# Four images through attention on one Trainium2 core: an image's head projections move up one output block, and the last LayerNorm is done in halves

## The chip, the cores and the metric

The kernel runs on one core of a Trainium2 chip. Times are microseconds (us) of device time for one launch, the median of several runs; the trace is that of one profiled execution.

## The reference

Four images of 256 channels and 32 x 32 pixels (N = 1024 tokens each) pass through three layers. Cut to what matters here:

```
q, k, v = wq x, wk x, wv x                     # layer 0: one attention of 1024 x 1024 per image
x = gamma * (v softmax(q^T k, axis=1)) + x
t = tokens(x)                                  # [4, 1024, 256]
h = groupnorm(layernorm(t)) * scale + bias     # layer 1: LayerNorm per token, GroupNorm per 8 channels
qkv = h w_qkv + b_qkv                          # 8 heads of 32
t = t + layernorm(t) + attention(q, k, v) w_proj + b_proj
t = t + expert(layernorm(t))                   # layer 2: one of 8 experts per token
```

Every softmax needs the maxima of its score rows before the exponentials; the kernel computes each score twice, once for the maxima and once for the exponentials.

## The kernel before, in words

The program is a sequence of four phases, each a block with its own instruction streams for TensorE (PE), VectorE (DVE), ScalarE (ACT), GpSimd (POOL) and the DMA queue of SyncE (SP). A phase starts when all engines have left the one before. The order in which each engine works is written out by hand, and semaphores (`wait_ge`) keep the engines apart; an engine works its stream in that order. `conv_phase` (layer 0 of all images, and layer 1 up to q, k and v), `head_phase` (32 attentions, four images times eight heads), `output_phase` and `expert_phase` follow each other.

In `conv_phase` a token block is 128 tokens, and an image has NB = 8 of them. For image b the stages are: `project` (q and k), `maxima` (8 blocks, two matmuls each into `ps_m`, reduced by DVE), `max_turn` (the maxima are transposed, and ACT and two small transfers put them as a row under the stacked keys), `scores` with ACT's exponentials, and then the output loop: `outputs(b, j)` for j = 0 to 7, eight matmuls into `ps_v`, after which DVE's `residual(b, j)` divides, adds the input and takes the LayerNorm statistics of the block. After the loop DVE's `first_norm(b)` normalizes all eight blocks into `lnt`.

Two other works are woven into image b's output loop. One is the next image's `maxima(b + 1, j)`, one block per j. The other is the layer-1 work of the image before, b - 1, by two tables, `precedes` and `follows`, indexed by j: `norms` part 0 (transposition of `lnt` into `ps_e`, statistics for GroupNorm), part 1 and part 2 (two tiny matmuls with `gmat` that sum over the channels of a group, each between short DVE chains that end in the scale and shift `gab`), ACT's `heads_in` (the normalized `h_c`, its rounded copy `h_hi`), DVE's `split_h` (the rest, `h_lo`), four `heads_qk` of 12 matmuls each, whose results ACT (`hi`) and DVE (`lo`) take from `ps_e` and SP spills to `qk_scr`, and two `heads_v` (48 matmuls in all), stored to `v_scr`. For the last image nothing follows, so this work is done after the loop (`last_image`), one part after another, and between the parts stand the first 14 (`LEAD`) blocks of maxima of head 0 and head 1 of the head phase (`hd.maxima`, `hd.block_max`); their operands, image 0's heads 0 and 1, are loaded during image 2's loop. Each `hd.maxima` waits until DVE has reduced the block before it, for it writes the same two banks of `ps_m`.

The tables of before, on PE:

```
precedes = {2: [(norms, 1)], 3: [(norms, 2)]}
follows = {0: [(norms, 0)], 5: [(heads_qk, 0), (heads_qk, 1)], 6: [(heads_qk, 2), (heads_qk, 3)],
           7: [(heads_v, 0), (heads_v, 1)]}
```

Of the kernel before, what the change touches and what calls it, by code (L numbers as in the profile page):

```python
# [27 lines left out]
ALU = mybir.AluOpType  # L28
# [88 lines left out]
def layer_norm(nc, st, done, lnt, res, mv, var, rstd, tmp):  # L117

    st.did(nc.vector.tensor_scalar(var[:, :], mv[:, :, 1], LN_EPS, None, ALU.add))
    st.wait()  # L120
    rsqrt(nc, st, rstd[:, :], var[:, :], tmp[:, :])
    for j in range(NB):
# [5 lines left out]
def moments(nc, st, mv, bst, pause):  # L128


    st.wait()
    nc.vector.memset(pause[:, :], 0.0)
    for j in range(NB):
        st.did(nc.vector.bn_aggr(mv[:, j, :], bst[:, j, :]))
# [119 lines left out]
def conv_phase(nc, io, keep, hd):  # L254
# [5 lines left out]
    with ExitStack() as ctx:  # L260
# [50 lines left out]
        a_whi, v_wlo, a_hhi, v_hlo = sem("a_whi", "v_wlo", "a_hhi", "v_hlo")  # L311
        PIECES = 4

        HEAD_BLOCKS = (2, 2, 2, 2, 2, 1, 1, 1, 1)
        assert sum(HEAD_BLOCKS) == LEAD

# [11 lines left out]
        with nc.Block() as block:  # L328

            @block.sync  # L330
            def _(sp):
# [103 lines left out]
            def _(act):  # L435
# [32 lines left out]
                def heads_in(b):  # L468

                    act.wait_ge(v_gab, b + 1)  # L470
# [5 lines left out]
                    for t in range(CT):  # L476
                        nc.scalar.activation(h_c[:, t, :], flat(ps_e[t]), ACT.Identity,
                                             scale=gab[:, 0, t:t + 1], bias=gab[:, 1, t:t + 1]).then_inc(a_h, 1)
                        act.wait_ge(a_h, 2 * b + t + 1)
                        nc.scalar.activation(h_hi[:, t, :], h_c[:, t, :], ACT.Copy).then_inc(a_hhi, 1)  # L480
                    for it in range(4):
                        if b == B - 1 and it == 3:
                            hd.row_hi(act, ps_v[:, 0, :], 0, 0, first=True)
# [26 lines left out]
            def _(pe):  # L510
# [87 lines left out]
                def norms(b, part):  # L598
# [5 lines left out]
                    else:  # L604

                        if b + 2 < B:
                            pe.wait_ge(v_max, 2 * (NB * (b + 2) + part + 1))
                        elif b == B - 1:
                            pe.wait_ge(hd.v_max, 2 * sum(HEAD_BLOCKS[:part]))
# [5 lines left out]
                def heads_qk(b, it):  # L615

                    pe.wait_ge(a_hhi, 2 * b + 2)
                    if b == 0 and it == 0:
# [39 lines left out]
                for b in range(-1, B):  # L658
                    for j in range(NB if b >= 0 else 0):
# [4 lines left out]
                        if b + 1 < B and not (b and j == NB - 1):  # L664
                            maxima(b + 1, j)
                        if b and b + 1 < B and j == NB - 1:
# [16 lines left out]
                last_image = [(norms, n) for n in range(3)] + [(heads_qk, n) for n in range(4)] + [(heads_v, n) for n in range(2)]  # L683
                for i, (part, n) in enumerate(last_image):
                    part(B - 1, n)
                    first = sum(HEAD_BLOCKS[:i])
                    for g in range(first, first + HEAD_BLOCKS[i]):
                        if g % NB == 0:
                            pe.wait_ge(*hd.loaded(hd.stack_in, 16 * STACK_DMAS, 0, g // NB))
                        if g == 0:  # L690
                            pe.wait_ge(v_max, 2 * NB * B)
                        hd.maxima(pe, ps_m, g, g // NB, g % NB, first=(g == 0))
                    if (part, n) == (heads_qk, 2):

                        pe.wait_ge(v_res0, NB * B)
                        hd.max_turn(pe, ps_v[:, 0, :], ident, 0, 0)

            @block.vector
            def _(dve):
# [46 lines left out]

                def first_norm(b):
# [46 lines left out]
                def split_h(b):  # L794

                    for t in range(CT):
                        dve.wait_ge(a_hhi, 2 * b + t + 1)
                        if b:
# [20 lines left out]
                precedes = {2: [(norms, 1)], 3: [(norms, 2)]}  # L819
                follows = {0: [(norms, 0)], 4: [(lambda b, n: split_h(b), 0)], 5: [(heads_qk, 0), (heads_qk, 1)], 6: [(heads_qk, 2), (heads_qk, 3)],  # L820
                           7: [(heads_v, 0), (heads_v, 1)]}
# [8 lines left out]
                for b in range(B):  # L830
                    for j in range(NB):
# [14 lines left out]
                    first_norm(b)  # L846
                    if b + 2 < B:
                        project(b + 2)
                last_image = [(norms, n) for n in range(3)] + [(heads_qk, n) for n in range(4)] + [(heads_v, n) for n in range(2)]
                for i, (part, n) in enumerate(last_image):  # L850
                    part(B - 1, n)
                    first = sum(HEAD_BLOCKS[:i])
                    for g in range(first, first + HEAD_BLOCKS[i]):
# [996 lines left out]
```

## Time and profile before

| | |
|---|---|
| median of 3 runs | 1238.78 us (1238.21 to 1240.36) |
| the profiled execution | 1240.58 us, its span 1238.8 us |
| PE busy | 1124.2 us, 91% of the span |
| DVE busy | 676.7 us, 55% |
| POOL busy | 570.6 us, 46% |
| ACT busy | 434.1 us, 35% |
| mean granted TensorE clock | 0.945 of full speed |

The shares are means over four phases; the change lies in the first, which ends at about 352.8 us of the span. The profile's own chain of waits, followed back from the end, does not reach that far, so the stage has to be read from the timelines of its engines.

### The profile page before, as it was taken

How to read it: one execution, taken by the hardware profiler on the slowest of the kernel's cores; microseconds unless marked ns; L12 is line 12 of the kernel's file. 1: busy time of each engine (PE TensorE's matmuls, PEld its weight loads, DVE VectorE, ACT ScalarE, POOL GpSimd, SP SyncE). 2: the span in 40 equal slices, each digit the busy share in tenths (PEclk: the TensorE clock that was granted, in tenths of full speed). 3: DMA queues.
4: the chain of work that ended last, by engine and by line, in shares of the span. 5: the costliest groups of instructions: out<-in, count | busy, mean ns of one | idle time of the engine just before them, and what ended most of it. 6: DMA issues, size and time to landing. Idle time of an engine off the chain costs nothing. (4 is left out here: it accounts for less than half of the span.)

```text
span 1238.8 us, 23452 instructions
## 1 busy us (share of the span) xinstructions
PE 1124.2 (91%) x7604; PEld 822.3 (66%) x7605; DVE 676.7 (55%) x1491; ACT 434.1 (35%) x511; POOL 570.6 (46%) x565
## 2 busy tenths in 40 slices
PE   6899999896679999999999999998726999999995
PEld 3577878685455555555555555556516999999994
DVE  4264747556467777777777777715742333333331
ACT  1303232320225555555555555564420111111110
POOL 0003030303047777877787878840361444444443
PEclk8799999897689999999999999998857999999998
DMA  6204361323152232323232323134455565565551
GB/s 210 60 1 128 135 188 68 119 87 131 73 167 76 80 94 60 94 60 94 60 94 67 101 68 100 31 121 136 149 118 175 194 215 193 191 203 208 191 193 61
DMA packets 61608, 148.44 MB, mean 120 GB/s; under 512 B 11360, under 2 KB 31776, under 8 KB 59904
## 3 DMA queue, kind: packets, MB, share of 16 engines
q1 hardware_dynamic: 53184, 123.39, 31.1%
q0 software_dynamic: 7536, 22.96, 5.6%
q10 hardware_dynamic: 848, 1.58, 0.5%
q8 instruction: 23, 0.38, 0.1%
q14 instruction: 17, 0.14, 0.0%
HBM read 104.58 MB, written 39.87 MB: 117 GB/s over the span
## 5 line engine op out<-in xcount | busy, mean ns | idle before, releaser
L217 DVE TENSOR_REDUCE s_nmax<-ps_v 128x1 f32<-128x512 f32 x484 | 311.3, 685 | 114.2 <-PE ps_v L211 104.0
L967 POOL TENSOR_TENSOR h_added<-h_added,h_expd 128x1024 f32<-128x1024 f32 x124 | 295.5, 2383 | 37.6 <-ACT h_expd L990 29.7
L990 ACT ACTIVATE h_expd<-ps_v 128x1024 f32<-128x1024 f32 x128 | 131.1, 1025 | 155.5 <-PE ps_v L1016 150.0
L1713 PEld LDWEIGHTS ps_h<-xs_c,lnt 128*128 128x128 f32 x1248 | 147.0, 194 | 4.8 <-issue 2.9
L1713 PE MATMUL ps_h<-xs_c,lnt 128*128 128x128 f32 x1248 | 147.5, 277 | 2.3 <-DVE xs_c L1665 2.3
L1723 PE MATMUL ps_y<-w,vals_t 128*128 x624 | 141.2, 379 | 0.6 <-DVE ys L1678 0.6
L1030 PE MATMUL h_ps_o<-h_expd,s_vh 128*32 128x256 f32 x2048 | 137.8, 387 | 0.0
L424 POOL TENSOR_TENSOR a_res<-a_res,a_lnt 128x2048 f32<-128x2048 f32 x4 | 18.2, 4539 | 253.0 <-DVE a_lnt L123 253.0
L990 ACT ACTIVATE h_expd<-h_ps_e 128x1024 f32<-128x1024 f32 x128 | 130.3, 1018 | 0.0
L1754 ACT ACTIVATE vals_t<-ps_h 128x1024 f32<-128x1024 f32 x39 | 39.9, 1024 | 255.8 <-DVE ps_h L1658 255.8
L1723 PEld LDWEIGHTS ps_y<-w,vals_t 128*128 128x128 f32 x624 | 115.5, 190 | 15.1 <-issue 1.0
L594 PE MATMUL a_ps_v<-a_val,a_expd 128*128 128x257 f32 x512 | 120.2, 388 | 5.1 <-ACT a_expd L464 4.5
L1658 DVE TENSOR_TENSOR ps_h<-ps_h,b_t 128x1024 f32<-128x1024 f32 x39 | 48.1, 1232 | 130.3 <-PE ps_h L1713 130.3
L594 PEld LDWEIGHTS a_ps_v<-a_val,a_expd 128*128 128x128 f32 x512 | 98.2, 194 | 23.5 <-ACT a_expd L464 6.5
L1555 POOL TENSOR_TENSOR pause<-pause 128x1 f32<-128x1 f32 x156 | 30.6, 196 | 156.0 <-DVE ys L1678 131.5
L967 POOL TENSOR_TENSOR h_added<-h_expd 128x1024 f32<-128x1024 f32 x31 | 73.8, 2380 | 56.2 <-ACT h_expd L990 56.2
L1030 PEld LDWEIGHTS h_ps_o<-h_expd,s_vh 128*32 128x32 f32 x2048 | 53.7, 109 | 52.0 <-issue 22.5
L715 DVE TENSOR_REDUCE a_nmax<-a_ps_m 128x1 f32<-128x512 f32 x64 | 41.2, 685 | 62.7 <-PE a_ps_m L554 62.7
L211 PE MATMUL ps_v<-s_stk2m,s_stk2n 96*128 96x512 f32 x128 | 51.9, 453 | 3.2 <-issue 3.1
L1176 POOL DMA_INDIRECT xs_scr<-lnt,pos x32 | 31.4, 982 | 50.6 <-DVE pos L1417 41.4
L211 PE MATMUL ps_v<-s_stk3m,s_stk3n 96*128 96x512 f32 x128 | 51.4, 446 | 0.0
L211 PE MATMUL ps_v<-s_stk1m,s_stk1n 96*128 96x512 f32 x116 | 46.6, 446 | 0.0
(222 smaller groups left out, 1592.2 us busy)
## 6 DMA issues: line engine op xcount, KB each, us to landing
lnt<-in_w SPq DMA_DIRECT2D x38, 1024.0 KB, 4.9
qk_scr<-a_head_hi SPq DMA_DIRECT2D x16, 512.0 KB, 2.6
qk_scr<-a_head_lo SPq DMA_DIRECT2D x16, 512.0 KB, 3.6
w<-in_w SPq DMA_DIRECT2D x8, 1024.0 KB, 5.9
xs<-xs_scr SPq DMA_DIRECT2D x39, 128.5 KB, 2.1
a_x_t<-in_x_t POOLq DMA_DIRECT2D x4, 1024.0 KB, 9.2
r_scr<-a_res POOLq DMA_DIRECT2D x4, 1024.0 KB, 6.1
v_scr<-res SPq DMA_DIRECT2D x4, 1024.0 KB, 3.8
```

Source lines behind the costliest of these rows:

```text
L211: self.nc.tensor.matmul(ps_m[:, half, :], n_st[0:STACK, nb * P:(nb + 1) * P], m_st[0:STACK, half * HALF:(half + 1) * HALF], start=True, st ...
L217: self.nc.vector.tensor_reduce(self.nmax[k][:, nb, half:half + 1], ps_m[:, half, :], AX.X, ALU.max, negate=True).then_inc(self.v_max, 1)
L594: last = nc.tensor.matmul(ps_v[:, j % 2, 0:C + 1], expd[:, m, j * P:(j + 1) * P], val[b % 2][:, m, :], start=(m == 0), stop=(m == NB - 1))
L715: nc.vector.tensor_reduce(nmax[b % 2][:, nb, half:half + 1], ps_m[:, half, :], AX.X, ALU.max, negate=True).then_inc(v_max, 1)
L967: nc.gpsimd.tensor_tensor(total[:, :], (expd[:, 0, :] if m == 1 else total[:, :]), expd[:, m, :], ALU.add).then_inc(g_add, 1)
L990: nc.scalar.activation(expd[:, m, :], flat(ps_e[m % 2]), ACT.Exp, scale=SCALE).then_inc(a_exp, 1)
L1030: mm = nc.tensor.matmul(ps_o[j % 2][q * D:(q + 1) * D, 0:QUARTER], vh[j % SLOTS][:, m, :], expd[:, m, q * QUARTER:(q + 1) * QUARTER], star ...
L1176: pool.indirect_dma_start(io["xs_scr"][:, :], bass.IndirectOffsetOnAxis(ap=keep["pos"][:, i:i + 1], axis=0), keep["lnt"][:, i, :], None).t ...
L1658: nc.vector.tensor_tensor(blocks, blocks, b1_t[:, bass.ds(e, 1), :].rearrange("p o (k n) -> p (o k) n", n=1).to_broadcast([P, KC, P]), ALU ...
L1713: last = nc.tensor.matmul(ps_h[k][:, c // 4, c % 4 * P:(c % 4 + 1) * P], w1_now[k][:, t, c * P:(c + 1) * P], xs_c[:, t, :], start=(t == 0) ...
L1723: last = nc.tensor.matmul(ps_y[:, 0:C], hid_t[k][:, c, :], w2[:, bass.ds(e, 1), c, :].rearrange("p o n -> p (o n)"), start=(c == 0), stop= ...
L1754: nc.scalar.activation(hid_t[k].rearrange("p k n -> p (k n)"), flat(ps_h[k]), ACT.Gelu).then_inc(a_gelu, 1)
```

## The change

Five edits, all in `conv_phase`:

- The layer-1 work of image b - 1 moves up one output block of image b: `norms` 1 and 2 stand before j = 1 and 2 instead of 2 and 3, `heads_qk` after j = 4 and 5, `heads_v` after j = 6 instead of 7; DVE's `split_h` after j = 3.
- The last image's `first_norm` becomes two halves of four token blocks: `norm_half(0)` on DVE after j = 5 of its own output loop, `norm_half(1)` after the loop; PE transposes each half on its own (`turn_half`).
- The eight blocks of head 0's maxima move from behind the last image's loop into it, one after each of j = 0 to 5 and two after j = 6 (`HEAD_BLOCKS`). Head 1's six blocks stay behind the loop: two after `norms` 2, one after each `heads_qk` (`TAIL_BLOCKS`). Head 0's row of maxima is therefore finished earlier, and SP writes it before the last image's first spill instead of before its fourth.
- ACT computes the rounded tile `h_hi` from PSUM with the same scale and shift as `h_c`, not as a copy of `h_c`, and before it; `heads_qk` 0 and 1 now also wait for `h_c`, which reads the bank that they overwrite.
- The waits before `norms` 1 and 2 are renumbered for the new places.

```diff
-def layer_norm(nc, st, done, lnt, res, mv, var, rstd, tmp):
+def layer_norm(nc, st, done, lnt, res, mv, var, rstd, tmp, blocks=range(NB)):
...
-        HEAD_BLOCKS = (2, 2, 2, 2, 2, 1, 1, 1, 1)
+        HEAD_BLOCKS = (1, 1, 1, 1, 1, 1, 2, 0)
+        TAIL_BLOCKS = {("norms", 2): 2, ("qk", 0): 1, ("qk", 1): 1, ("qk", 2): 1, ("qk", 3): 1}
+        HALVES = (range(0, NB // 2), range(NB // 2, NB))
...
-                        if b == B - 1 and it == 3:
+                        if b == B - 1 and it == 0:
                             hd.max_rows(sp, 0, 0)
...
-                        nc.scalar.activation(h_c[:, t, :], flat(ps_e[t]), ACT.Identity,
-                                             scale=gab[:, 0, t:t + 1], bias=gab[:, 1, t:t + 1]).then_inc(a_h, 1)
-                        act.wait_ge(a_h, 2 * b + t + 1)
-                        nc.scalar.activation(h_hi[:, t, :], h_c[:, t, :], ACT.Copy).then_inc(a_hhi, 1)
+                        for h, done in ((h_hi, a_hhi), (h_c, a_h)):
+                            nc.scalar.activation(h[:, t, :], flat(ps_e[t]), ACT.Identity,
+                                                 scale=gab[:, 0, t:t + 1], bias=gab[:, 1, t:t + 1]).then_inc(done, 1)
...
+                def turn_half(half):
+                    pe.wait_ge(*((v_lnh, 1), (v_ln, B))[half])
+                    if half == 0:
+                        pe.wait_ge(v_v1, 2 * (B - 1))
+                    for t in range(CT):
+                        for j in HALVES[half]:
+                            last = nc.tensor.transpose(ps_e[t][:, half, j % 4 * P:(j % 4 + 1) * P], lnt[:, j, t * P:(t + 1) * P], ident[:, :])
+                        last.then_inc(pe_lnh, 1)
...
-                precedes = {2: [(norms, 1)], 3: [(norms, 2)]}
-                follows = {0: [(norms, 0)], 5: [(heads_qk, 0), (heads_qk, 1)], 6: [(heads_qk, 2), (heads_qk, 3)],
-                           7: [(heads_v, 0), (heads_v, 1)]}
+                precedes = {1: [(norms, 1)], 2: [(norms, 2)]}
+                follows = {0: [(norms, 0)], 4: [(heads_qk, 0), (heads_qk, 1)], 5: [(heads_qk, 2), (heads_qk, 3)],
+                           6: [(heads_v, 0), (heads_v, 1)]}
...
+                        if b == B - 1:
+                            head_blocks(sum(HEAD_BLOCKS[:j]), HEAD_BLOCKS[j])
...
+                turn_half(0)
+                pe.wait_ge(v_res0, NB * B)
+                hd.max_turn(pe, ps_v[:, 0, :], ident, 0, 0)
+                turn_half(1)
...
+                def norm_half(half):
+                    b, blocks = B - 1, HALVES[half]
+                    moments(nc, st, mv, bst, pause, blocks)
+                    st.wait()
+                    if half == 0:
+                        dve.wait_ge(g_res, 2 * b - 1)
+                    layer_norm(nc, st, (v_lnh, v_ln)[half], lnt, res[b % 2], mv, var, rstd, tmp, blocks)
...
+                        if b == B - 1 and j == NB // 2 + 1:
+                            norm_half(0)
-                    first_norm(b)
+                    if b + 1 < B:
+                        first_norm(b)
```

On DVE in the last image's loop, from the `lo` parts of the last two `heads_qk` to the reductions of head 0's blocks. Before, the LayerNorm of the whole image stands behind the loop:

```order
L806 SCALAR_TENSOR_TENSOR a_head_lo<-a_ps_e,a_b_qk,a_head_hi 128x1024 x2
L738 RECIPROCAL a_rc<-a_ps_v 128x1
L740 TENSOR_TENSOR a_rg<-a_rc,a_gamma 128x1
L742 SCALAR_TENSOR_TENSOR a_res<-a_ps_v,a_rg,a_x_t 128x256
L745 BN_STATS a_bst<-a_res 128x6
L814 TENSOR_TENSOR res<-a_ps_e,a_b_v 128x4x8x32 x2
L132 MEMSET a_pause 128x1
L134 BN_AGGR a_mv<-a_bst 128x2 x8
```

In the changed kernel, at the same place:

```order
L853 SCALAR_TENSOR_TENSOR a_head_lo<-a_ps_e,a_b_qk,a_head_hi 128x1024 x2
L133 MEMSET a_pause 128x1
L135 BN_AGGR a_mv<-a_bst 128x2 x4
L120 TENSOR_SCALAR a_var<-a_mv 128x4
...
L124 TENSOR_SCALAR a_lnt<-a_res,a_mv,a_rstd 128x256 x4
L218 TENSOR_REDUCE s_nmax<-a_ps_m 128x1 x4
L228 TENSOR_REDUCE s_nmaxes<-s_nmax 128x8
L769 RECIPROCAL a_rc<-a_ps_v 128x1
```

The whole first half of the LayerNorm (11 small steps stand where the dots are) now comes between the last `lo` and the four reductions of head 0's blocks 6 and 7.

On PE at the end of image 2's loop, before: the last maxima, the last outputs, the turn of the maxima, then `heads_v` (24 rows of this form, one shown) and the scores of image 3:

```order
L554 MATMUL a_ps_m<-a_stk1m,a_stk1n 128x512 x2
L594 MATMUL a_ps_v<-a_val,a_expd 128x257 x8
L564 MATMUL a_ps_v<-ident,a_msplit 16x128
L640 MATMUL a_ps_e<-a_w_v_hi,a_h_hi 128x256 x2
...
L579 MATMUL a_ps_e<-a_stk1n,a_stk1m 128x512 x16
```

And now:

```order
L646 MATMUL a_ps_e<-a_w_v_hi,a_h_lo 128x256 x2
L557 MATMUL a_ps_m<-a_stk1m,a_stk1n 128x512 x2
L597 MATMUL a_ps_v<-a_val,a_expd 128x257 x8
L567 MATMUL a_ps_v<-ident,a_msplit 16x128
L582 MATMUL a_ps_e<-a_stk1n,a_stk1m 128x512 x16
```

The turn of the maxima and the scores that need its row are now neighbours; `heads_v` stands ahead of both.

On PE behind the last image's loop, before (after the last `heads_v` of image 2, which is the first row):

```order
L640 MATMUL a_ps_e<-a_w_v_hi,a_h_lo 128x256 x2
L140 MATMUL a_ps_e<-ident,a_lnt 128x128 x16
L211 MATMUL a_ps_m<-s_stk0m,s_stk0n 128x512 x4
L611 MATMUL a_ps_m<-a_mvc,a_gmat 128x2
L211 MATMUL a_ps_m<-s_stk0m,s_stk0n 128x512 x4
L611 MATMUL a_ps_m<-a_gw,a_gmat 128x2
L211 MATMUL a_ps_m<-s_stk0m,s_stk0n 128x512 x4
L628 MATMUL a_ps_e<-a_h_hi,a_w_qk_hi 128x512 x4
```

And now (the first row is the last output group):

```order
L597 MATMUL a_ps_v<-a_val,a_expd 128x257 x8
L658 MATMUL a_ps_e<-ident,a_lnt 128x128 x8
L233 MATMUL a_ps_v<-ident,s_nmaxes 8x128
L658 MATMUL a_ps_e<-ident,a_lnt 128x128 x8
L614 MATMUL a_ps_m<-a_mvc,a_gmat 128x2
L614 MATMUL a_ps_m<-a_gw,a_gmat 128x2
L212 MATMUL a_ps_m<-s_stk1m,s_stk1n 128x512 x4
L634 MATMUL a_ps_e<-a_h_hi,a_w_qk_hi 128x512 x4
```

Two blocks of maxima (four matmuls) stand ahead of the first `heads_qk` where six stood.

## Rows read from the trace of the kernel before

**Rows 1.** Stretches: us; busy PE, PEld, DVE, ACT, POOL (instructions); PE clock, DMA, GB/s.
```profile
228.90:283.50 54.60, 51.10 (x214) 40.11 (x215) 27.52 (x90) 16.87 (x16) 9.94 (x3) 0.91 0.25 98
283.50:352.80 69.30, 45.79 (x194) 34.71 (x192) 42.78 (x99) 9.02 (x9) 9.94 (x3) 0.75 0.28 109
```
**Rows 2.** PE's timeline from image 3's last outputs on: start, duration, line, count, [idle].
```profile
279.89 3.64 PE L594 MATMUL a_ps_v<-a_val,a_expd 128*128 128x257 f32 x16
...
296.23 3.67 PE L140 MATMUL a_ps_e<-ident,a_lnt 128*128 128x128 f32 x16 [7.01 <-DVE a_lnt L123]
...
316.92 2.07 PE L628 MATMUL a_ps_e<-a_h_hi,a_w_qk_hi 128*128 128x512 f32 x4 [2.51 <-ACT a_h_hi L480]
...
324.88 1.39 PE L211 MATMUL a_ps_m<-s_stk0m,s_stk0n 96*128 96x512 f32 x2 [2.65 <-DVE s_nmax L217]
...
339.97 1.18 PE L628 MATMUL a_ps_e<-a_h_hi,a_w_qk_hi 128*128 128x512 f32 x4
...
342.86 1.00 PE L211 MATMUL a_ps_m<-s_stk1m,s_stk1n 96*128 96x512 f32 x2
...
352.87 0.31 PE L1009 MATMUL h_ps_o<-ident 128*128 128x128 f32 x1 [2.32 <-PEq L328]
```
**Rows 3.** PE's timeline, image 2's loop and the joint to image 3's.
```profile
175.73 3.75 PE L594 MATMUL a_ps_v<-a_val,a_expd 128*128 128x257 f32 x16 [1.11 <-ACT a_expd L464]
...
181.53 3.64 PE L594 MATMUL a_ps_v<-a_val,a_expd 128*128 128x257 f32 x16
...
222.48 0.28 PE L564 MATMUL a_ps_v<-ident,a_msplit 128*16 128x128 f32 x1 [0.37 <-DVE a_msplit L729]
...
228.00 0.40 PE L640 MATMUL a_ps_e<-a_w_v_hi,a_h_lo 128*128 128x256 f32 x2
229.76 1.16 PE L579 MATMUL a_ps_e<-a_stk1n,a_stk1m 98*128 98x512 f32 x4 [1.36 <-issue]
...
239.50 5.13 PE L594 MATMUL a_ps_v<-a_val,a_expd 128*128 128x257 f32 x16 [1.11 <-ACT a_expd L464]
```
**Rows 4.** PE's timeline at image 0's end, and the same place among PEld's waits.
```profile
89.82 0.28 PE L564 MATMUL a_ps_v<-ident,a_msplit 128*16 128x128 f32 x1 [1.76 <-DVE a_msplit L729]
...
93.60 1.20 PE L579 MATMUL a_ps_e<-a_stk1n,a_stk1m 98*128 98x512 f32 x4
...
PEld a_ps_e L579 <- DMA a_stk1n<-a_mrow: 0.8, 1, 0.8
```
**Rows 5.** DVE's timeline: image 1's group statistics in image 2's loop.
```profile
184.84 0.15 DVE L765 BATCH_NORM_AGGREGATE a_mvc<-a_gst 128x2 f32<-128x12 f32 x1
```
**Rows 6.** DVE's timeline from the last `heads_qk` of image 2 to the phase's end.
```profile
281.24 1.28 DVE L806 SCALAR_TENSOR_TENSOR a_head_lo<-a_ps_e,a_b_qk,a_head_hi 128x1024 fp32r<-128x1024 f32 x1 [1.52 <-ACT a_head_hi L488]
...
284.48 0.43 DVE L745 BATCH_NORM_STATS2 a_bst<-a_res 128x6 f32<-128x256 f32 x1
...
290.50 0.54 DVE L134 BATCH_NORM_AGGREGATE a_mv<-a_bst 128x2 f32<-128x6 f32 x7
...
293.50 2.67 DVE L123 TENSOR_SCALAR a_lnt<-a_res,a_mv,a_rstd 128x256 f32<-128x256 f32 x8
...
299.94 1.29 DVE L761 BATCH_NORM_STATS2 a_gst<-a_ps_e 128x6 f32<-128x512 f32 x2 [0.41 <-PE a_ps_e L140]
...
304.85 0.16 DVE L769 COPY a_mg<-a_ps_m 128x2 f32<-128x2 f32 x1 [0.68 <-PE a_ps_m L611]
...
309.44 0.16 DVE L778 TENSOR_SCALAR a_var<-a_ps_m 128x2 f32<-128x2 f32 x1 [0.68 <-PE a_ps_m L611]
...
351.27 1.28 DVE L217 TENSOR_REDUCE s_nmax<-a_ps_m 128x1 f32<-128x512 f32 x2
```
**Rows 7.** TensorE's granted clock (third figure from the end) in one stretch.
```profile
331.00:332.00 1.00, 0.79 (x3) 0.29 (x2) 0.00 (x0) 0.64 (x1) 0.00 (x0) 0.95 0.00 0
```
**Rows 8.** ACT's timeline: the first activation behind the last image's `gab`.
```profile
312.39 1.20 ACT L477 ACTIVATE a_lnt<-a_ps_e,a_gab 128x1024 f32<-128x1024 f32 x1 [31.19 <-DVE a_gab L786]
```
**Rows 9.** SP's queue: the store of the last image's values.
```profile
351.38 0.33 SPq L373 DMA_DIRECT2D v_scr<-res  x1
```

More of the change, by code:

```diff
@@ L125, in layer_norm, with moments @@
     last.then_inc(done, 1)
-def moments(nc, st, mv, bst, pause):
+def moments(nc, st, mv, bst, pause, blocks=range(NB)):
     st.wait()
     nc.vector.memset(pause[:, :], 0.0)
-    for j in range(NB):
+    for j in blocks:
         st.did(nc.vector.bn_aggr(mv[:, j, :], bst[:, j, :]))
@@ L606, in norms @@
                         if b + 2 < B:
[L607 to L609 removed]
+                            pe.wait_ge(v_max, 2 * (NB * (b + 2) + part))
+                        else:
+                            pe.wait_ge(hd.v_max, 2 * (part if b < B - 1 else NB))
                         pe.wait_ge(*((v_gst, 2 * b + 2), (v_gdev, b + 1))[part - 1])
@@ L682, in _ @@
                                 values_piece(b + 2, m - 1)
[L683 to L696, printed above, removed]
+                turn_half(0)
+                pe.wait_ge(v_res0, NB * B)
+                hd.max_turn(pe, ps_v[:, 0, :], ident, 0, 0)
+                turn_half(1)
+                done = NB
+                for n in (1, 2):
+                    norms(B - 1, n)
+                    more = TAIL_BLOCKS.get(("norms", n), 0)
+                    head_blocks(done, more)
+                    done += more
+                for n in range(4):
+                    heads_qk(B - 1, n)
+                    more = TAIL_BLOCKS.get(("qk", n), 0)
+                    head_blocks(done, more)
+                    done += more
+                for n in range(2):
+                    heads_v(B - 1, n)
             @block.vector
@@ L817, in heads_v, with head_blocks @@
                                             ALU.add).then_inc(v_v1, 1)
-                precedes = {2: [(norms, 1)], 3: [(norms, 2)]}
-                follows = {0: [(norms, 0)], 4: [(lambda b, n: split_h(b), 0)], 5: [(heads_qk, 0), (heads_qk, 1)], 6: [(heads_qk, 2), (heads_qk, 3)],
-                           7: [(heads_v, 0), (heads_v, 1)]}
+                def head_blocks(first, n):
+                    for g in range(first, first + n):
+                        hd.block_max(dve, ps_m, g, g // NB, g % NB)
+                        if g == NB - 1:
+                            hd.least(dve, 0, 0, first=True)
+                precedes = {1: [(norms, 1)], 2: [(norms, 2)]}
+                follows = {0: [(norms, 0)], 3: [(lambda b, n: split_h(b), 0)], 4: [(heads_qk, 0), (heads_qk, 1)], 5: [(heads_qk, 2), (heads_qk, 3)],
+                           6: [(heads_v, 0), (heads_v, 1)]}
                 project(0)
@@ L845, in _ @@
                                 split_max(b + 1)
-                    first_norm(b)
+                        if b == B - 1 and j == NB // 2 + 1:
+                            norm_half(0)
+                    if b + 1 < B:
+                        first_norm(b)
                     if b + 2 < B:
                         project(b + 2)
[L849 to L853, printed above, removed]
-                        if (part, n) == (norms, 2) and g == first + 1:
-                            split_h(B - 1)
-                        hd.block_max(dve, ps_m, g, g // NB, g % NB)
-                        if g == NB - 1:
-                            hd.least(dve, 0, 0, first=True)
-                    if (part, n) == (heads_qk, 2):
-                        hd.row_lo(dve, ps_v[:, 0, :], 0, 0)
+                norm_half(1)
+                hd.row_lo(dve, ps_v[:, 0, :], 0, 0)
+                done = NB
+                for n in range(3):
+                    norms(B - 1, n)
+                    more = TAIL_BLOCKS.get(("norms", n), 0)
+                    head_blocks(done, more)
+                    done += more
+                split_h(B - 1)
+                for n in range(4):
+                    heads_qk(B - 1, n)
+                    more = TAIL_BLOCKS.get(("qk", n), 0)
+                    head_blocks(done, more)
+                    done += more
+                for n in range(2):
+                    heads_v(B - 1, n)
 def head_phase(nc, io, keep, sems, hd):
```

38 lines of the change are left out of this document (29 added, 9 removed).

## Prediction

> **What bounds the stage now.** I read the stretches first, then PE's timeline behind the last loop, then DVE's and ACT's at the idle times it shows. While image 3's exponentials and loop run (228.9 to 283.5), PE is busy 51.1 of 54.6 us: PE is the bound. In the 69.3 us behind the loop (283.5 to 352.8) it is busy 45.8 us at a granted clock of 0.75, DVE 42.8 us, ACT 9.0 us: nobody is full, and a chain that passes from engine to engine is the bound [rows 1]. Its links: the last output group ends at 279.89 + 3.64 = 283.53 (I call this time T); PE stands still for 7.01 us until DVE's LayerNorm is done, transposes at 296.23, and reaches the first `heads_qk` only at 316.92, T + 33.4; after that 2.65 us waits for DVE's reductions come back, as at 324.88; the head phase's first matmul is at 352.87, T + 69.3 [rows 2]. Work taken out of this chain and put into the loop costs its PE time there and nothing else, as long as the loop stays PE's.
>
> **The joint between images 2 and 3 (+2.0, image 1's end -0.2).** The maxima are turned at 222.48, `heads_v` ends at 228.40, scores start at 229.76, 7.28 after the turn: `heads_v` hides the way of the row (ACT, two transfers). Now `heads_v` comes first; the turn starts 5.9 later, less the 0.37 it waits now, at 228.0 [rows 3]. Nothing stands between it and the scores, since image 4 doesn't exist and there is no `project`. What the row's way costs is seen at image 0's end: turn at 89.82, scores at 93.60, 3.78 later, and PE's weight load waited for the row's transfer there [rows 4]. So scores start at 231.8 instead of 229.76: +2.0, bounds 1.5 and 2.5. At image 1's end `project` still covers the row, and 0 to 0.37 of waiting goes.
>
> **The loops of images 1 to 3, shifted (0).** The sequence of the layer-1 parts is the same, one block earlier. The one place with less room is `norms` 1, now behind the second output group: in image 2's loop that group ends at 181.53 + 3.64 = 185.17 [rows 3], and DVE has the statistics at 184.99 [rows 5], so the wait is hidden by 0.2 us; if it were not, some 0.3 us per image. ACT's `h_hi` from PSUM is priced as the 1.20 of `h_c` [rows 8]; the new waits for `h_c` end while `outputs` run.
>
> **Image 3's loop (+9.6 without a stall).** It takes 283.53 - 239.50 = 44.0 us now, of which 1.4 is a first group at half clock (5.13 against 3.75). Image 2's loop is the same with eight blocks of maxima more: 175.73 to 222.11 (222.48 less the wait), 46.4 us [rows 2, 3]. Eight blocks so cost 46.4 - 42.6 = 3.7. `heads_v`, now ahead of the last outputs, costs the 5.9 above.
>
> **The new stall in it (+4.1).** At j = 6 PE has outputs 6, then head 0's blocks 6 and 7. Block 7 writes the banks that block 6 fills, so it waits for DVE's reductions of block 6, and on DVE these stand behind `norm_half(0)`. Counted from X, the end of the last `heads_qk` (279.89 in the present loop): the last `lo` ends at 282.52, X + 2.6 [rows 2, 6]. The whole LayerNorm goes from 290.50 (seven aggregations in 0.54) to 293.50, then 2.67 for eight blocks [rows 6]; a half is about 2.7 of aggregation and small steps, with 1.34 of normalizing: 4.1. So reductions start at X + 6.7; a pair takes 1.28 [rows 6], and block 7's second matmul can go at X + 8.0, `heads_v` at X + 8.3. Without the wait it would be X + 4.2 (an output group of 3.64, overlapped by some 0.3, and two blocks of 0.47). Queued behind block 7 are `heads_v`, outputs 7 and the whole tail. Bounds: 0, if DVE came early, and 4.5.
>
> **The clock after the stall (+1.9).** PE is idle for some 3.6 us at j = 6. After 1.36 us of idle time four score matmuls take 1.16 us, full clock (229.76) [rows 3]; after 2.65 us (324.88) the clock stays low until the second that begins at 331, with 0.95 [rows 2, 7], 6 us; after 7.01 us it is low too: sixteen transpositions take 3.67 [rows 2]. So 3.6 us lies on the low side; I take 4 us of dense work at half clock, half of it extra: 2 less what the idle part takes, 1.9; bounds 0 and 3. The Trainium skill's page "TensorE: Matmul & The Clock Gate", in its section "What's actually happening", says that the throttled state is the default and activity releases it, and that where the change falls isn't tied to the kernel's start. By that rule the lower bound, 0, is unlikely; the sum would be the one below.
>
> T moves by 2.0 - 0.2 + 3.7 + 5.9 + 4.1 + 1.9 = **17.4 us**, to 300.9.
>
> **The tail, from T to the head phase (69.3 becomes 41.3).** DVE's last residual is done at 284.48 + 0.43, T + 1.4; `norm_half(1)` takes 4.1, T + 5.5; `row_lo` 0.3; then the statistics, each pair 1.29: the first half's turned tiles are there, the second half's eight transpositions end at T + 7.4 (half of 3.67), so both pairs end at T + 8.3, with their aggregation T + 8.6 [rows 2, 6]. Each group sum costs 0.7 (0.68 of DVE waiting), the chain between them 0.9 (four steps of 0.16 and their gaps), the last chain 2.9 (309.44 to ACT's start at 312.39) [rows 6, 8]: `gab` at T + 13.8, now T + 28.9. No block of maxima stands among them any more. PE may start behind three of ACT's four activations (4.53 from 312.39 to 316.92 for four, so 3.5): the first `heads_qk` at T + 17.3 instead of T + 33.4. It runs mostly at half clock, as it does now (2.07 for its first four matmuls, 1.18 at full clock): 4.9. Then full clock, since the waits are short: a `heads_qk` is 342.86 - 339.97 = 2.9, its block 0.5, and some 0.6 of each block is a wait for DVE, which does a `lo` of 1.28 and a pair of reductions of 1.28 per step [rows 2, 6]. 17.3 + 4.9 + 0.5 + 3 x 3.5 = 33.2; `heads_v` 5.9: 39.1; DVE's last add 1.2: 40.3. Now the end is DVE's last reduction, 351.27 + 1.28 = 352.55, and the head phase starts 0.32 later. Then SP's store stood well before the end (351.38, issue 0.33) [rows 9]; now it stands at the end and adds its 0.33, and competes longer with the head phase's first loads: 0 to 0.9. Together T + 41.3. GpSimd's two additions and their store start at T + 5.5 and are covered by the rest; SP's row of maxima waits for T + 5.8, long before the first spill.
>
> Sum: the head phase starts at 300.9 + 41.3 = 342.2 instead of 352.87, **10.6 us earlier**. The phases behind it are untouched, so the profiled execution would take 1240.58 - 10.6 = 1230.0. That execution lies 1.8 above the median of the runs, 1238.78; the median becomes **1228.2**.
>
> **Rivals.**
> - *No stall at block 7* (15 in 100). If DVE were through with the half norm in time, 4.1 and 1.9 stay away: 16.6 gained, 1222.2. For it: DVE is busy only 27.5 of 54.6 us in the loop [rows 1]. Against it: the order of its rows is fixed, and the 4.1 us stand between `lo` and the reductions whatever its load.
> - *A dearer tail* (17 in 100). The clock stays low longer, behind the stall and through `heads_qk` 1, or each block waits the 2.65 seen at 324.88: 4 to 6 us of the gain go, about 1233.
> - *Nothing comes of it* (4 in 100). If all that leaves the tail returned in the loop, as added PE work and waits, the time is 1238.8. Against it: PE is idle for 23.5 of 69.3 us in the tail and at 0.75 of its clock, and that idle time is not moved with the work.
> - *Slower* (4 in 100). The stall lets the clock fall, and it stays at half through `heads_v`, outputs 7, three `heads_qk` and the last `heads_v`: 5.9 + 3.3 + 8.7 + 5.9 = 23.8 extra, less the 1.9 counted: 1250. It decides from 10.6 us of extra, some 21 us of full-clock work. Against it: in rows with dense work the low clock lasted 6 us.
>
> The forecast has the rest, 60 in 100, with its own range 1225.5 to 1231. To leave out no more than 2 in 10, the range reaches to the stall's absence below and the dear tail above: **1222 to 1233.5**. A measurement of this kernel can tell some 0.2%, 2.5 us, from no change. Faster holds the forecast, the first two rivals and a little of the rest: 0.93; within 0.2%: 0.03; slower: 0.04.
>
> **What the new profile would show.** The scores of image 3 some 9.3 us behind the place of the present turn, with PE idle about 3.4; in image 3's loop one PE idle time of 3 to 4 us ahead of a block of head 0, put down to the reductions; the last output group ending near 301; `gab` about 14 behind it; the first `heads_qk` 17 behind it; the head phase near 342. The prediction is wrong if block 7 does not wait, if ACT or the group sums wait for something else behind T (GpSimd's addition, which ACT awaits, is due at about T + 10, `gab` at T + 13.8), or if the later phases move.

## Result: faster by 0.55%, less than forecast

| | before | changed | ratio, 95% interval |
|---|---|---|---|
| median, 20 runs each | 1241.66 us | 1234.84 us | 0.9945 (0.9931 to 0.9958) |
| profiled execution, its span | 1240.58, 1238.8 us | 1232.84, 1231.0 us | |

The change is worth 6.8 us of medians; 10.6 were forecast, and 1234.84 lies above the range. Of the distance from 1228.2, 3.8 us are gain that did not come, and 2.9 us are the base: 1238.78 was the median of three runs, 1241.66 is that of twenty. Either part alone would have left the time inside the range. The two profiled spans differ by 7.8 us: the head phase starts 6.04 us earlier (352.87, now 346.83), and the phases behind it, whose code is unchanged, took 1.76 us less; over the thirteen profiled executions of this document they took 882.9 to 885.9.

The stretches of the stage, now divided at T' = 296.69 + 3.64 = 300.33 (below, T stands for each kernel's own end of its last output group), answer to [rows 1]; the columns are the same.

```profile
229.30:300.30 71.00, 63.97 (x278) 51.27 (x279) 42.01 (x120) 16.71 (x16) 9.95 (x3) 0.88 0.25 98
300.30:346.80 46.50, 28.30 (x130) 21.55 (x129) 32.87 (x72) 9.22 (x9) 9.90 (x4) 0.78 0.32 125
```

The loop has grown as forecast; the tail fell from 69.3 to 46.5 us, but not to 41.3. PE's timeline of the changed kernel, which answers to [rows 2, 3]:

```profile
227.00 0.27 PE L567 MATMUL a_ps_v<-ident,a_msplit 128*16 128x128 f32 x1
230.16 1.21 PE L582 MATMUL a_ps_e<-a_stk1n,a_stk1m 98*128 98x512 f32 x4 [2.88 <-DMA a_stk1n<-a_mrow]
...
239.94 6.35 PE L597 MATMUL a_ps_v<-a_val,a_expd 128*128 128x257 f32 x16 [1.11 <-ACT a_expd L468]
...
281.15 3.64 PE L597 MATMUL a_ps_v<-a_val,a_expd 128*128 128x257 f32 x16
284.44 0.81 PE L212 MATMUL a_ps_m<-s_stk0m,s_stk0n 96*128 96x512 f32 x2
288.54 1.10 PE L212 MATMUL a_ps_m<-s_stk0m,s_stk0n 96*128 96x512 f32 x2 [3.28 <-DVE s_nmax L218]
289.48 0.49 PE L646 MATMUL a_ps_e<-a_w_v_hi,a_h_hi 128*128 128x256 f32 x2
...
293.13 0.40 PE L646 MATMUL a_ps_e<-a_w_v_hi,a_h_hi 128*128 128x256 f32 x2
...
296.69 3.64 PE L597 MATMUL a_ps_v<-a_val,a_expd 128*128 128x257 f32 x16
...
305.98 1.32 PE L658 MATMUL a_ps_e<-ident,a_lnt 128*128 128x128 f32 x8 [4.41 <-DVE a_lnt L124]
...
315.24 0.56 PE L614 MATMUL a_ps_m<-a_gw,a_gmat 128*128 128x2 f32 x2 [5.71 <-DVE a_gw L821]
...
322.28 2.08 PE L634 MATMUL a_ps_e<-a_h_hi,a_w_qk_hi 128*128 128x512 f32 x4 [1.44 <-ACT a_h_hi L484]
...
346.83 0.30 PE L1072 MATMUL h_ps_o<-ident 128*128 128x128 f32 x1 [2.26 <-PEq L332]
```

Of the long waits, 2.88 at the joint, 3.28 ahead of head 0's block 7 and 4.41 ahead of the second half's transpositions were forecast; 5.71 ahead of the second group sum was not. DVE's timeline there, answering to the group sums of [rows 6], and POOL's beside it:

```profile
304.54 1.38 DVE L124 TENSOR_SCALAR a_lnt<-a_res,a_mv,a_rstd 128x256 f32<-128x256 f32 x4
...
309.63 0.16 DVE L815 COPY a_mg<-a_ps_m 128x2 f32<-128x2 f32 x1 [0.81 <-PE a_ps_m L614]
309.82 0.69 DVE L817 TENSOR_TENSOR a_gdev<-a_mvc,a_mg 128x2 f32<-128x2 f32 x1
310.55 0.16 DVE L819 TENSOR_TENSOR a_gdev<-a_gdev 128x2 f32<-128x2 f32 x1
310.75 4.34 DVE L821 TENSOR_TENSOR a_gw<-a_gdev,a_mvc 128x2 f32<-128x2 f32 x1
315.83 0.16 DVE L824 TENSOR_SCALAR a_var<-a_ps_m 128x2 f32<-128x2 f32 x1 [0.74 <-PE a_ps_m L614]
...
318.63 0.16 DVE L832 TENSOR_TENSOR a_gab<-a_gnw,a_tmp 128x2 f32<-128x2 f32 x1
```
```profile
306.00 4.50 POOL L428 TENSOR_TENSOR a_res<-a_res,a_lnt 128x2048 f32<-128x2048 f32 x1 [61.22 <-DVE a_lnt L124]
310.58 4.50 POOL L430 TENSOR_TENSOR a_res<-a_res,a_b_pr 128x2048 f32<-128x2048 f32 x1
```

An addition of two numbers per partition takes 4.34 us, where its neighbour takes 0.16. It is booked as busy time, not as a wait. It ends at 315.09, GpSimd's second addition at 315.08; `a_gdev` ends at 310.51, the first addition at 310.50.

**The other rows that answer.** ACT's first activation behind `gab` now starts at 318.83 ([rows 8]: 312.39). SP's store of the values is issued at 345.85 ([rows 9]: 351.38).

### The profile page after: what moved, and what is told of

Its sections match the earlier page's. It is cut to its first block and busy times, and to the rows that moved or that the text cites. A ratio compares the mean times of both kernels' runs of the same rounds, so it can differ in the third digit from the quotient of the medians.

```text
span 1231.0 us, 23475 instructions
## 1 busy us (share of the span) xinstructions
PE 1115.7 (91%) x7604; PEld 817.6 (66%) x7605; DVE 683.5 (56%) x1504; ACT 433.9 (35%) x511; POOL 570.0 (46%) x565
## 5 line engine op out<-in xcount | busy, mean ns | idle before, releaser
L1721 DVE TENSOR_TENSOR ps_h<-ps_h,b_t 128x1024 f32<-128x1024 f32 x39 | 48.1, 1233 | 130.7 <-PE ps_h L1776 130.7
```

Source lines behind the costliest of these rows:

```text
L1721: nc.vector.tensor_tensor(blocks, blocks, b1_t[:, bass.ds(e, 1), :].rearrange("p o (k n) -> p (o k) n", n=1).to_broadcast([P, KC, P]), ALU ...
```

## Theory, rival and how the runs are compared

Theory (**the port**): while a GpSimd addition runs, some VectorE operations that read SBUF stand still until it is over. The change puts the chain between the group sums under the additions; before, they were nearly over (below). Rivals: the 4.34 us belong to the operation itself or to a wait booked on it; or taking the hold away only moves the time elsewhere.

Spans of one kernel differ by several us from execution to execution, so the table shows stretches within the profiled executions (start of one image's scores to the next, to T, to the head phase), and the ratio of all runs to those of the kernel before. Apart from e10, only e6, e7 and e11 have a ratio whose interval lies clear of the changed kernel's; for the others the stretches decide.

| kernel | image 2's stretch | image 3's scores to T | T to head phase | ratio (95%) |
|---|---|---|---|---|
| before | 67.02 | 53.77 | 69.34 | 1 |
| changed | 68.24 | 70.17 | 46.50 | 0.9945 (0.9931 to 0.9958) |
| e1 late bias | 69.93 | 70.49 | 46.54 | 0.9951 (0.9930 to 0.9972) |
| e2 additions on one block | 68.25 | 70.11 | 41.99 | one run, 1226.09 us |
| e3 one input | 68.24 | 70.15 | 45.50 | 0.9926 (0.9909 to 0.9942) |
| e4 two at 5 | 69.94 | 66.26 | 46.74 | 0.9916 (0.9891 to 0.9940) |
| e5 old joint | 67.93 | 70.42 | 46.62 | 0.9948 (0.9932 to 0.9965) |
| e6 halves | 68.24 | 70.30 | 42.67 | 0.9891 (0.9873 to 0.9908) |
| e7 halves, two at 5 | 69.94 | 66.23 | 41.67 | 0.9874 (0.9855 to 0.9894) |
| e8 split joint | 66.76 | 70.41 | 46.58 | 0.9934 (0.9912 to 0.9957) |
| e9 copied `h_hi` | 69.93 | 70.48 | 47.33 | 0.9934 (0.9908 to 0.9961) |
| e10 shift alone | 68.27 | 60.37 | 64.20 | 1.0015 (1.0004 to 1.0026) |
| e11 all three | 66.76 | 66.28 | 41.76 | 0.9858 (0.9830 to 0.9886) |

## Experiments on the tail

**e1, the bias later.**

```diff
                     pool.wait_ge(g_res, 2 * b + 1)
+                    if b == B - 1:
+                        pool.wait_ge(v_hlo, 2 * B)
                     nc.gpsimd.tensor_tensor(r[:, :, :], r[:, :, :], over_blocks(b_pr[:, :], NB), ALU.add).then_inc(g_res, 1)
```

> For the last image GpSimd's second addition (the bias) starts only when h is split; its first one stays where it is. Port theory (VectorE's operation with two SBUF inputs stands until GpSimd's addition is over): the last weight a_gw takes some 0.16 us instead of 4.34, a_gdev keeps its 0.5 to 0.7 because the first addition still lies over it; gab comes some 4.2 us earlier after the last output group (14.3 us instead of 18.5), the head phase starts some 42.3 us behind the last output group instead of 46.5, and the time is about 4 us below the changed kernel's. Rival, that the 4.34 us come from the operation itself or from a wait that the profile books there (the chain of small steps, a semaphore): a_gw keeps about 4.3 us and the time stays. Second rival, that the wait only moves: something else takes GpSimd's place (its late addition runs over the heads' reductions, or its store of the residual comes late for the head phase), so that gab is early and the head phase is not.

`a_gw` fell to 0.16 and was done before the bias began, so it had waited for no result of it; `a_gdev`, still under the first addition, kept 0.52 and ended with it. The first `heads_qk` came at T + 17.73 instead of 21.95. The head phase did not move: 46.54. The bias now runs from 322.45, and the store of the residual, issued at 327.30, meets the heads' spills. ACT's and PE's timeline of e1:

```profile
335.09 1.11 ACT L493 ACTIVATE a_head_hi<-a_ps_e,a_b_qk 128x1024 fp32r<-128x1024 f32 x1 [4.93 <-DMA qk_scr<-a_head_lo]
```
```profile
338.17 1.09 PE L212 MATMUL a_ps_m<-s_stk1m,s_stk1n 96*128 96x512 f32 x2 [2.13 <-DVE s_nmax L218]
```

and the DMA issues of this part of the program, first of the changed kernel, then of e1 (last figure: median us from issue to landing):

```profile
qk_scr<-a_head_lo SPq DMA_DIRECT2D x4, 512.0 KB, 3.9
r_scr<-a_res POOLq DMA_DIRECT2D x1, 1024.0 KB, 5.1
```
```profile
qk_scr<-a_head_lo SPq DMA_DIRECT2D x4, 512.0 KB, 5.4
r_scr<-a_res POOLq DMA_DIRECT2D x1, 1024.0 KB, 7.4
```

ACT waits 4.93 us for a spill to free its buffer and the 4.2 us are given back: the hold is the additions' doing, and the second rival holds for this remedy. That it is the store, and not the addition ahead of it, that slows the spills is read from these times; no run separates the two.

**e2, the additions on one block of eight.**

```diff
+                    nb = slice(0, NB if b < B - 1 else 1)
-                    nc.gpsimd.tensor_tensor(r[:, :, :], r[:, :, :], lnt[:, :, :], ALU.add).then_inc(g_res, 1)
+                    nc.gpsimd.tensor_tensor(r[:, nb, :], r[:, nb, :], lnt[:, nb, :], ALU.add).then_inc(g_res, 1)
```

(and the bias in the same way; seven of the last image's eight blocks go without both additions)

> GpSimd's two additions of the last image are done on one of its eight blocks only (so the residual of seven blocks of the last image lacks the LayerNorm and the bias). Port theory: both a_gdev and a_gw take some 0.16 us, gab some 4.7 us earlier behind the last output group (13.8 us, as forecast), head phase some 41.8 us behind it instead of 46.5. Rival, that the two durations have another cause: they stay at about 0.7 and 4.3 us.

DVE's timeline of e2:

```profile
307.38 0.16 DVE L816 COPY a_mg<-a_ps_m 128x2 f32<-128x2 f32 x1 [0.81 <-PE a_ps_m L615]
307.58 0.16 DVE L818 TENSOR_TENSOR a_gdev<-a_mvc,a_mg 128x2 f32<-128x2 f32 x1
307.77 0.16 DVE L820 TENSOR_TENSOR a_gdev<-a_gdev 128x2 f32<-128x2 f32 x1
307.97 0.16 DVE L822 TENSOR_TENSOR a_gw<-a_gdev,a_mvc 128x2 f32<-128x2 f32 x1
```

Both are 0.16. `gab` is there at T + 13.9 (forecast 13.8) and the tail is 41.99 (forecast 41.3): with the additions out of the way the forecast's tail stands, within 0.7 us.

**e3, one streamed input.**

```diff
+                            nc.vector.tensor_tensor(gdev[:, :], mvc[:, :, 0], sums, ALU.subtract).then_inc(v_gd1, 1)
...
+                            for t in range(CT):
+                                last = nc.vector.tensor_scalar(gw[:, t:t + 1], gdev[:, t:t + 1], gdev[:, t:t + 1], mvc[:, t, 1:2], ALU.mult, ALU.add)
```

> GpSimd's two additions stay where they are. For the last image VectorE gets a_gdev from a_mvc and the sums in PSUM, and a_gw by two tensor_scalar operations whose other operands are one number per partition, so that no operation of that chain streams two SBUF inputs. Port theory, if the lock holds only for two streamed SBUF inputs: the chain from the first sum to the last takes about 1.3 us under GpSimd's additions instead of 5.5, the time some 4 us less than the changed kernel's. If the lock holds for any VectorE operation of this chain that reads SBUF: some of them still end with GpSimd's additions and nothing is won. Rival without a port: no difference from the changed kernel beyond one instruction.

DVE's timeline of e3; GpSimd's additions run from 305.05 to 309.55 and from 309.63 to 314.13:

```profile
308.68 0.16 DVE L824 TENSOR_TENSOR a_gdev<-a_mvc,a_ps_m 128x2 f32<-128x2 f32 x1 [0.81 <-PE a_ps_m L614]
...
309.02 0.45 DVE L829 TENSOR_SCALAR a_gw<-a_gdev,a_mvc 128x1 f32<-128x1 f32 x2
310.21 0.16 DVE L833 TENSOR_SCALAR a_var<-a_ps_m 128x2 f32<-128x2 f32 x1 [0.74 <-PE a_ps_m L614]
310.41 3.75 DVE L80 TENSOR_SCALAR a_tmp<-a_var 128x2 int32<-128x2 int32 x1
```

The rewritten steps pass freely under the additions; then a `tensor_scalar` with one SBUF input and constants stands still for 3.75 us, to 314.16. So the hold is not on two inputs alone, and moving it one step on returned 1.0 us of the tail, not 4. The Trainium skill's page "SBUF — State Buffer", section "Who interferes with whom", has a cause for this: VectorE and GpSimd share a pair of ports under a lock that lasts a whole instruction, and it is needed by a VectorE operation with two SBUF inputs against a GpSimd operation that reads SBUF, and by `tensor_scalar` in a mode that uses both ports. The traces agree in three rows: 4.34 for two inputs, 0.16 with one of them in PSUM, 3.75 for the `tensor_scalar`. What the runs show is the hold and which operations it meets; that it is a port, and that this `tensor_scalar` ran in such a mode, no trace shows.

**e6, the additions by halves.**

```diff
+                    if b == B - 1:
+                        nb, n2 = slice(NB // 2, NB), NB // 2
+                        pool.wait_ge(v_lnh, 1)
+                        nc.gpsimd.tensor_tensor(r[:, 0:n2, :], r[:, 0:n2, :], lnt[:, 0:n2, :], ALU.add).then_inc(g_half, 1)
...
+                        nc.gpsimd.tensor_tensor(r[:, 0:n2, :], r[:, 0:n2, :], over_blocks(b_pr[:, :], n2), ALU.add).then_inc(g_half, 1)
```

> GpSimd's two additions of the last image are split: the first four blocks get theirs as soon as the first half's norm is done, inside the output loop, the last four behind the second half's norm as now. Port theory: behind norm_half(1) GpSimd is busy for some 4.5 us instead of 9, until about the end of a_gdev; a_gdev keeps 0.7 us or less, a_gw falls from 4.34 to some 0.2, gab comes some 4.2 us earlier behind the last output group, and the store of the residual now starts some 4.5 us earlier, so that it does not meet the spills of the heads: head phase some 42.3 us behind the last output group instead of 46.5, the time some 4 us below the changed kernel's. Rival: the additions of the first half hold VectorE up inside the loop by as much (its reductions or the residual stand still for 2 to 4 us while PE waits there), so that the last output group ends 2 to 4 us later and half or more of it is lost.

POOL's and DVE's timeline of e6:

```profile
288.22 2.39 POOL L434 TENSOR_TENSOR a_res<-a_res,a_b_pr 128x1024 f32<-128x1024 f32 x1
303.89 2.35 POOL L437 TENSOR_TENSOR a_res<-a_res,a_lnt 128x1024 f32<-128x1024 f32 x1 [13.28 <-DVE a_lnt L124]
306.32 2.34 POOL L439 TENSOR_TENSOR a_res<-a_res,a_b_pr 128x1024 f32<-128x1024 f32 x1
```
```profile
288.49 2.13 DVE L780 TENSOR_TENSOR a_rg<-a_rc,a_gamma 128x1 f32<-128x1 f32 x1
...
307.83 0.85 DVE L826 TENSOR_TENSOR a_gdev<-a_mvc,a_mg 128x2 f32<-128x2 f32 x1
308.71 0.16 DVE L828 TENSOR_TENSOR a_gdev<-a_gdev 128x2 f32<-128x2 f32 x1
308.90 0.16 DVE L830 TENSOR_TENSOR a_gw<-a_gdev,a_mvc 128x2 f32<-128x2 f32 x1
```

In the loop the second addition holds up a residual's second step (`a_rg`) for 2 us, to its own end (290.62 and 290.61), and PE, busy with `heads_v`, does not notice: the loop takes 70.30 against 70.17. In the tail only 0.7 us of hold is left, and the tail is 42.67, 3.8 shorter; the rival, that the loop loses as much, is refuted. By the ratios e6 is 0.54% below the changed kernel, some 6.7 us; the two intervals leave 2.9 to 10.5, so the trace's 3.8 is the better figure.

## Experiments on the loop and the joint

**e4, the double block one group earlier.**

```diff
-        HEAD_BLOCKS = (1, 1, 1, 1, 1, 1, 2, 0)
+        HEAD_BLOCKS = (1, 1, 1, 1, 1, 2, 1, 0)
```

> In image 3's loop head 0's two blocks at once stand behind output group 5 instead of 6 (the table reads 1,1,1,1,1,2,1,0), so no block of maxima waits for reductions behind the first half's norm. Stall theory (block 7 waits for DVE's reductions, which stand behind the half norm): the wait of 3.3 us in front of block 7 and the low clock behind it (1.6 us) go, a pair wait of about 0.9 us at group 5 comes; the last output group ends 4 to 5 us earlier (about 296 instead of 300.3), the time falls by some 4 to 5 us. Rival, that reductions behind the half norm make the same wait elsewhere (heads_v of the image or max_turn waits for them instead): the last output group moves by less than 1.5 us.

PE's timeline of e4:

```profile
279.01 0.81 PE L212 MATMUL a_ps_m<-s_stk0m,s_stk0n 96*128 96x512 f32 x2
280.38 1.10 PE L212 MATMUL a_ps_m<-s_stk0m,s_stk0n 96*128 96x512 f32 x2 [0.56 <-DVE s_nmax L218]
...
290.21 0.82 PE L212 MATMUL a_ps_m<-s_stk0m,s_stk0n 96*128 96x512 f32 x2
```

0.56 us of waiting takes the place of 3.28, and the stretch from image 3's scores to T falls from 70.17 to 66.26. This profiled execution had lost 3.8 us ahead of image 3, so its T is not earlier in absolute time (300.21); the stretch shows the edit. The ratio points the same way, 0.29% below the changed kernel's, but the two intervals overlap.

**e5, the old joint.** In image 2's loop `heads_v` goes back behind the turn, on PE and on DVE:

```diff
-                            for part, n in follows.get(j, ()):
+                            for part, n in follows.get(j - 1 if b == B - 2 and j >= NB - 1 else -1 if b == B - 2 and j == NB - 2 else j, ()):
```

> In image 2's loop alone heads_v and the turn of image 3's maxima stand in the order of before again (turn first, then heads_v). Joint theory: the idle time of 2.88 us in front of image 3's scores goes, and 1.5 to 2.5 us of the end of image 3's loop with it: the time 2 us below the changed kernel's. Rival, that the wait returns in another place (heads_v, now later, fills time that the row's way would have hidden anyway, or image 3's exponentials wait for ACT): less than 1 us.

The stretch fell by 0.3 us only, to 67.93. The wait for the row went, but ahead of image 3's scores PE still stands idle for 1.36 us, as before the change [rows 3]:

```profile
228.41 1.16 PE L582 MATMUL a_ps_e<-a_stk1n,a_stk1m 98*128 98x512 f32 x4 [1.36 <-issue]
```

and with `heads_v` gone from between them, maxima 6 and 7 stand back to back: the second waits 0.56 for its bank, and the pair takes 1.2 us longer. 2.88 - 1.36 - 1.2 leaves the 0.3. The rival held.

**e8, `heads_v` split around the turn.**

```diff
+                            now = follows.get(j, ())
+                            if b == B - 2 and j >= NB - 2:
+                                now = [(heads_v, j - (NB - 2))]
```

> The changed kernel, but in image 2's loop only the first half of heads_v stands behind output group 6; the second half stands behind the turn of image 3's maxima, where its 2.9 us of matmuls lie beside the row's way (3.2 us from turn to scores). Joint theory (the row's way is uncovered there): the idle time of 2.88 us in front of image 3's scores falls to 1.4 us or less, image 2's stretch from scores to scores takes 65.5 to 67 us instead of 68.24, the time 1.5 to 2.5 us below the changed kernel's. Rival, as the run with the old joint showed (67.93 there): what goes at the joint comes back as a wait between maxima 6 and 7: less than 0.7 us.

PE's timeline of e8 at the scores of image 3 (ahead of it twelve rows of `heads_v` behind the turn at 225.20):

```profile
229.69 1.16 PE L582 MATMUL a_ps_e<-a_stk1n,a_stk1m 98*128 98x512 f32 x4 [1.36 <-issue]
```

Image 2's stretch is 66.76, 1.48 shorter, shorter than before the change too. The 1.36 us are the same idle time as in e5, put down to no transfer: half of `heads_v` is enough to cover the row, and the joint theory holds. The times alone (0.9934 against 0.9945) can't tell 1.5 us.

**e9, `h_hi` copied again.**

```diff
+                        act.wait_ge(a_h, 2 * b + t + 1)
+                        nc.scalar.activation(h_hi[:, t, :], h_c[:, t, :], ACT.Copy).then_inc(a_hhi, 1)
```

> The changed kernel, but ScalarE makes the rounded tile from h_c, behind a wait, as before, and not from PSUM. By the prediction's term (PE may start behind three of the four activations): the first heads_qk of the last image 1.0 to 1.4 us later behind gab, the loops of images 1 to 3 unchanged, the time 1.0 to 1.4 us above the changed kernel's. Rival: nothing, because the first heads_qk runs at half clock and other waits follow: less than 0.5 us.

The first `heads_qk` came at T + 23.03 instead of 21.95, 1.08 later, as the term says; the head phase 0.83 later behind T. The times (0.9934) can't tell so small an effect.

**e10, the shift alone on the kernel before** (both engines' tables and the renumbered wait):

```diff
-                precedes = {2: [(norms, 1)], 3: [(norms, 2)]}
+                precedes = {1: [(norms, 1)], 2: [(norms, 2)]}
...
-                            pe.wait_ge(v_max, 2 * (NB * (b + 2) + part + 1))
+                            pe.wait_ge(v_max, 2 * (NB * (b + 2) + part))
```

> The kernel before with nothing changed but the two tables: heads' work, norms and the split of an image one block earlier in the loops of images 1 to 3; the last image as before. Forecast by the prediction's terms: 2.0 lost at the joint of images 2 and 3, 0.2 won at image 1's end, nothing in the loops: 1.8 us slower than before, since nothing behind image 3's loop is changed (its last block gives heads_v away from the end and gets it one block earlier). Rival: the loops themselves get faster or slower by more than 1 us through the shift (norms 1 with less room).

1242.51 us against 1240.59, 1.0015 (1.0004 to 1.0026): the shift by itself costs about 1.9 us (0.5 to 3.2), and 1.8 was forecast. The trace does not confirm the split: image 2's stretch is 1.25 us longer (2.0 forecast), and image 3's scores to the head phase 1.46 longer (nothing forecast), so that the sum agrees is in part luck. None of the change's gain comes from the shift; it comes from the last image.

**e7 and e11, the remedies together.** e7 is e6 with e4's table, e11 is e7 with e8's split.

> GpSimd's additions split as in the run before, and head 0's double block behind output group 5 instead of 6. If both effects are separate they add: last output group 3.9 us earlier behind the scores of image 3 (as seen with the double block moved alone), tail 4.2 us shorter: the time some 8 us below the changed kernel's, 14 to 15 below the kernel before. If the moved block brings its reductions under GpSimd's additions or the norm of the first half starts later: only one of the two, some 4 us.

> GpSimd's additions split by halves, head 0's double block behind group 5, and heads_v split around the turn in image 2's loop. If the three effects add: 4.0 us of the stall, 4 to 5 us of the tail and 1.5 to 2.5 us of the joint less than the changed kernel, a time of 1223 to 1225 us, 16 us or more below the kernel before. If the joint gives nothing: 1225 to 1227 us, as with the first two alone.

The effects add: the loop of e4 (66.23 and 66.28), a tail of 41.67 and 41.76, the joint of e8 (66.76). The tails are 1.0 us shorter than e6's because the first `heads_qk` with its block took 4.79 us in e7 and 5.86 in e6: the granted clock rose earlier (mean 0.67 and 0.53). Tails compare to about 1 us for this reason. e7 takes 1225.35 us, e11 1222.2 us with the kernel before at 1241.98 beside it: 0.9858 (0.9830 to 0.9886), 17.6 us less than before and 10.8 less than the change; its three stretches are 10.1 us shorter than the change's. e11 is a version that beats both.

## Why the prediction was wrong

**The step that failed** is "GpSimd's two additions and their store start at T + 5.5 and are covered by the rest". They do start at T + 5.7 and nobody waits for their result, but VectorE, for which they count as cover, stands still under them. The term that it spoils is "the chain between them 0.9": from 309.63 to 315.09 it took 5.5. That is 4.6 of the 5.2 us by which the tail missed 41.3, and e2 shows the tail at 41.99 with all but an eighth of them left out. The prediction's own sign of being wrong, that the group sums wait for something else behind T, came true; it had GpSimd's addition in mind there only as something that ACT awaits.

The kernel before had the sign. DVE's and POOL's timeline of before, at the same chain:

```profile
305.04 0.34 DVE L771 TENSOR_TENSOR a_gdev<-a_mvc,a_mg 128x2 f32<-128x2 f32 x1
305.42 0.16 DVE L773 TENSOR_TENSOR a_gdev<-a_gdev 128x2 f32<-128x2 f32 x1
305.62 0.16 DVE L775 TENSOR_TENSOR a_gw<-a_gdev,a_mvc 128x2 f32<-128x2 f32 x1
```
```profile
300.86 4.51 POOL L426 TENSOR_TENSOR a_res<-a_res,a_b_pr 128x2048 f32<-128x2048 f32 x1
```

`a_gdev` took 0.34 where its equals take 0.16, and ended at 305.38, with the addition (305.37): the chain began just as the additions ended. The chain's price was read there as "four steps of 0.16", where it was nearly free of them. The change moves it 5 us closer to the end of the norm (8.7 us behind it before, 3.7 now), and so under them.

**What held.**
- T: +17.4 forecast. Counted from image 1's scores (93.60 before, 93.08 now), T came 17.3 later. Within it, image 1's stretch gave 0.3 (0.2), the joint cost 1.2 (2.0: the row's way took 3.16 from turn to scores, not 3.78; at image 0's end, where 3.78 was read, PE was busy with `project` from the turn to the scores, so that 3.78 is only an upper bound of the row's way), image 3 took 16.4 more (15.6), of which 1.2 is a first output group longer at half clock (6.35 against 5.13, at a mean granted clock of 0.58 against 0.72), which no term had.
- The stall: `heads_v` at X + 8.33 with X = 281.15, forecast 8.3. The clock behind it: `heads_v` rows at half clock to 293.13 (granted 0.51, and 1.00 behind it), about 1.5 extra, forecast 1.9. e4 takes 3.9 of the two back.
- The tail's other terms: `norm_half(1)` ends at T + 5.6 (5.5), the statistics at 8.5 (8.6), the last chain 3.0 (2.9), from ACT's start to the first `heads_qk` 3.45 (3.5), the half-clock `heads_qk` 5.1 (4.9), steps of 3.6 on average (3.5), `heads_v` 5.9.

**The rivals.** The stall came, so the first was out. "A dearer tail" had the size, 4 to 6 us and about 1233, by chance and not by its cause: neither the clock's part nor the waits per block grew by more than 0.3. No rival named the additions as a hold on VectorE.

## What to carry to other kernels

"Covered" needs two questions: who waits for the result, and whom does the covering work itself hold up. Before a VectorE chain is moved, look at what GpSimd does at the new place, and compare the durations of equal small operations: one that is longer than its twins and ends together with a GpSimd instruction was held here, and it was booked as busy, not as a wait. When work is moved off such a place, follow its stores too: in e1 the later store took back what the freed chain had won.

## What the runs showed of the hardware

- Under GpSimd's additions these VectorE operations stood still: 128x2 and 128x1 `tensor_tensor` with both inputs in SBUF (up to 4.34 and 2.13 us), a 128x2 int32 `tensor_scalar` (3.75). These did not: the reductions and statistics from PSUM, a copy and a 128x2 `tensor_tensor` with one input in PSUM (0.16), the aggregation with its one input in SBUF (0.20), and a 128x1 `tensor_scalar` whose operands are one number per partition (0.45 for two). Between two additions 0.08 us apart one operation got through (`a_gdev` at 310.55).
- Equal code takes two lengths. Image 2's first output group, behind the sparse scores, took 3.75 us in nine of thirteen profiled executions and about 5.43 in four (e1, e4, e7, e9), with image 2's stretch 1.7 us longer (69.94 against 68.24). Of the changed kernel and of e1:

```profile
174.90 3.75 PE L597 MATMUL a_ps_v<-a_val,a_expd 128*128 128x257 f32 x16 [1.11 <-ACT a_expd L468]
```
```profile
174.77 5.43 PE L599 MATMUL a_ps_v<-a_val,a_expd 128*128 128x257 f32 x16 [1.11 <-ACT a_expd L470]
```

The longer group has part of its matmuls at half clock (mean granted clock 0.69 in e1, 1.00 in the changed kernel). Image 1's first group shows the same two lengths, 3.75 in six executions and 5.2 to 5.4 in seven (these four, e8, e10 and e11), with its stretch some 1.5 us longer. What the engines are told to do up to there is the same in the changed kernel and in e1 and e4. This is why the stretches were compared image by image. Each kernel has one profiled execution, so whether such steps make up the spread of 7 to 9 us among one kernel's runs is not shown, and what decides between the two lengths was not settled.
